# Moving the edge sums behind the slot's node and sort steps, and deepening the load buffers, in a two-layer graph attention kernel

## What is computed

```python
for l in range(L):                                   # L = 2
    xn = _layernorm(x, ln1_g[l], ln1_b[l])
    deg = segment_sum(ones, src); deg = (deg - deg.mean()) / (std(deg, ddof=1) + 1e-06)
    pos = xn @ Wpos[l] + bpos[l] + deg[:, None] * Wdeg[l][0] + bdeg[l]
    xp = xn + pos
    q, k, v = (xp @ W + b).reshape(n, H, HD)         # Wq, Wk, Wv
    att = clip(einsum('ehd,ehd->eh', q[dst], k[src]) / sqrt(HD), -50, 50)
    ex = exp(att - segment_max(att, dst)[dst]); s = segment_sum(ex, dst)
    aggr = segment_sum(v[src] * (ex / (s[dst] + 1e-16))[:, :, None], dst)
    x = x + (aggr @ Wo[l] + bo[l])
    h = gelu(_layernorm(x, ln2_g[l], ln2_b[l]) @ W1[l] + b1[l], approximate=False)
    x = x + (h @ W2[l] + b2[l])
return _layernorm(x_in + x)
```

## Time and profile before

| | |
|---|---|
| three runs | 3809.2 us median (3791.64 to 3824.87) |
| the profiled execution | 3805.99 us, of which 3804.0 us is the span of its instructions |
| mean granted TensorE clock | 0.886 of full speed |
| busy in the span | PE 83%, DVE 76%, POOL 66%, ACT 48% |
| indirect DMAs of POOL | 2448 |
| prologue; gathers of layer 0; of layer 1; rest | 0 to 289; 289 to 2074; 2126 to 3748; to 3804 us |

### The profile page before, as it was taken

How to read it: one execution, slowest core, us unless ns; L and a number is a source line. 1 busy time by engine, 2 the same in 40 slices (tenths; PEclk the granted TensorE clock), 3 DMA queues, 4 the chain that set the end, 5 groups by cost and what they waited for, 6 DMA issues and landing times.

```text
span 3804.0 us, 74324 instructions
## 1 busy us (share of the span) xinstructions
PE 3174.2 (83%) x25705; PEld 2515.7 (66%) x25705; DVE 2900.9 (76%) x6187; ACT 1820.2 (48%) x4404; POOL 2523.6 (66%) x2470
## 2 busy tenths in 40 slices
PE   4984688889898888889898688888888888888887
PEld 3763467667676676767676476667766676666665
DVE  8985688788678878877887387777877777777776
ACT  1331255445444444544555345555555555555555
POOL 1007777777666767766676477777777767777773
PEclk7685699999899999989999699899999989998997
DMA  3015455455454545545454355555555555555552
GB/s 85 22 62 150 115 159 173 151 158 152 139 153 148 161 144 155 154 142 150 148 176 133 102 164 160 178 165 166 151 178 168 167 165 168 168 168 165 163 168 79
DMA packets 427249, 558.53 MB, mean 147 GB/s; under 512 B 78473, under 2 KB 345441, under 8 KB 426677
## 3 DMA queue, kind: packets, MB, share of 16 engines
q0 software_dynamic: 117504, 321.02, 28.4%
q1 hardware_dynamic: 301862, 225.47, 19.6%
q10 hardware_dynamic: 7506, 7.20, 0.6%
HBM read 527.98 MB, written 25.44 MB: 145 GB/s over the span
## 4 chain that ended last, share of the span: by engine, by line
PE 44%; DVE 26%; issue 8%; ACT 8%; POOL 7%; DMA 5%; SPq 2%; DVEq 1%; POOLq 0%; ACTq 0%
PE psum L951 12%; POOL kv_ring L1964 6%; PE psum L1041 5%; DVE att L1682 4%; PE psum L992 4%; PE psum L1025 3%; DVE scratch L1673 3%; PE psum L1062 3%; DVE work L1377 2%; PE psum L1008 2%; DVE kv_ring L1394 2%; PE psum L1122 2%; DMA arena<-kv_table 2%; DVE arena L1724 2%; DMA q_win<-q_table 2%
## 5 line engine op out<-in xcount | busy, mean ns | idle before, releaser
L1964 POOL DMA_INDIRECT kv_ring<-kv_table,src_idx x1840 | 1888.1, 1026 | 746.5 <-issue 543.4
L1227 ACT ACTIVATE scratch<-psum 128x512 f32<-128x512 f32 (+1 forms) x1228 | 678.1, 567 | 484.1 <-PE psum L961 305.3
L1964 POOL DMA_INDIRECT arena<-kv_table,src_idx x608 | 617.2, 1015 | 241.0 <-issue 178.0
L951 PE MATMUL psum<-arena 128*128 128x256 f32 x2156 | 677.8, 437 | 72.5 <-ACT scratch L1227 42.1
L1238 ACT COPY arena<-psum 128x512 f32<-128x512 f32 x616 | 327.1, 532 | 593.7 <-PE psum L951 578.6
L992 PE MATMUL psum<-q_win,scratch 64*128 64x128 f32 x4896 | 413.1, 316 | 160.5 <-DVE scratch L1673 80.4
L951 PEld LDWEIGHTS psum<-arena 128*128 128x128 f32 x2156 | 425.7, 218 | 179.8 <-ACT scratch L1227 57.8
L1682 DVE TENSOR_REDUCE att<-scratch 128x64 f32<-128x1024 f32 (+1 forms) x460 | 535.7, 1165 | 0.1
L992 PEld LDWEIGHTS psum<-q_win,scratch 64*128 64x128 f32 x4896 | 349.2, 215 | 262.8 <-issue 165.6
L1673 DVE TENSOR_TENSOR scratch<-psum,kv_ring 128x1024 f32<-128x1024 f32 x230 | 280.4, 1219 | 154.7 <-DMA kv_ring<-kv_table,src_idx 92.2
L1008 PE MATMUL psum<-scratch 128*64 128x136 f32 x4896 | 371.5, 296 | 31.9 <-ACT work L1321 11.5
(11 more groups left out here) (252 smaller groups left out, 4839.3 us busy)
## 6 DMA issues: line engine op xcount, KB each, us to landing
arena<-kv_table SPq DMA_DIRECT2D x154, 896.0 KB
kv_ring<-kv_table,src_idx POOLq DMA_INDIRECT x1840
q_win<-q_table SPq DMA_DIRECT2D x612, 32.0 KB
work<-kv_table SPq DMA_DIRECT2D x98, 128.0 KB
q_win<-q_table SPq DMA_DIRECT2D x154, 64.0 KB
arena<-kv_table,src_idx POOLq DMA_INDIRECT x608
work<-q_table SPq DMA_DIRECT2D x98, 64.0 KB
kv_table<-work SPq DMA_DIRECT2D x49, 128.0 KB, 2.0
```

The source lines that it names most:

```text
L951: mm = e.matmul(to[:, t % 2 * 2 * D:(t % 2 + 1) * 2 * D], hot_source[:, t * P:(t + 1) * P], source_rows[:, t, :], start=True, stop=True)
L1227: e.activation(to[:, at:at + width], apart[k % FILL_BANKS][:, 0:width], ACT.Relu, bias=1.0, scale=-1.0).then_inc(apart_read, 1)
L1964: e.indirect_dma_start(kv[m % RING_KV][:, t, :], None, kv_table[l], bass.IndirectOffsetOnAxis(ap=src_idx[:, c * T + t:c * T + t + 1], axis ...
```

## The change

1. In DVE's program `add_sums` of u - 1 stands behind the node and sort steps of slot 2u + 1, and no longer straight behind the messages.
2. `q_win` has 4 buffers for 2, `source_rows` 2 for 1, `plan_b` 3 for 2. The loads are issued 4 units, two blocks and 6 units (`BLOCK_AHEAD`) ahead.
3. Fills: the first two `rows` of unit u + 3 stand in slot 2u + 1 and the last two of u + 2 in slot 2u, each half one slot sooner than before; `source` of u + 4 stands at the end of slot 2u + 1.
4. The 23 steps of a sort are laid evenly between the end of the sort before and the slot by which they must be done. Layer 0's blocks begin at chunk 19, for 17.
5. `b_next` becomes a part of the three-row bf16 split, so its PE product is one bf16 matmul of 3 rows for a float32 one of 1 row; the five DVE operations of the split work on 1280 columns, for 896.
6. The arena grows by 2240 words a partition, and `dynamic_dma_scratch_size=8192` is given at the build, for the default of 16384. This is the part of each SBUF partition that holds the descriptors of POOL's DMAs. Some semaphores are merged.

```diff
-FIRST_B = 17, 4
+FIRST_B = 19, 4
+QUERIES = 4
+BLOCK_AHEAD = 6
+PLANS_B = 3
-ARENA = 16656
+ARENA = 18896
...
         for u in range(self.nu):
-            ahead = [("source", u + 3, h) for h in range(2) if self.is_block(u + 3)]
+            ahead = [("source", u + 4, h) for h in range(2) if self.is_block(u + 4)]
             turn = [("turn", u + 2, h) for h in range(self.parts_of(u + 2))] if u + 2 < self.nu else []
             hot = [("hot", u, h) for h in range(self.parts_of(u))]
-            rows = [[("rows", u + 2, i)] if self.is_block(u + 2) else [] for i in range(4)]
-            fills[2 * u] = turn[:1] + rows[0] + turn[1:] + rows[1] + ahead
-            fills[2 * u + 1] = hot[:1] + rows[2] + hot[1:] + rows[3]
+            rows = [[("rows", u + (3 if i < 2 else 2), i)] if self.is_block(u + (3 if i < 2 else 2)) else [] for i in range(4)]
+            fills[2 * u] = turn[:1] + rows[2] + turn[1:] + rows[3]
+            fills[2 * u + 1] = hot[:1] + rows[0] + hot[1:] + rows[1] + ahead
...
     for s in range(NBS[0]) if l == 0 else range(NBS[0], NBS[1]):
-        if l == 0:
-            u = max(u, 2 * at[(s - 1) * OB] - 8 if s else 0)
-        else:
-            u = max(u, 2 * at[(s - NBS[0]) * 3 * OB])
+        first, end = u, 2 * (at[s * OB] - BLOCK_AHEAD) - 2
         for k in range(SORT_STEPS):
+            u = max(u, first + k * (end - first) // SORT_STEPS)
...
-            u += SORT_EVERY if s and 5 <= k < SORT_STEPS - 4 else 1
+            u += 1
...
-        q_win = sb("q_win", [P, 2, D])
+        q_win = sb("q_win", [P, QUERIES, D])
-        b_next = sb("b_next", [P, QKV])
+        b_next = sb("b_next", [3, QKV], BF16)
-        source_rows = part_of(TB * 2 * D).rearrange("p (t d) -> p t d", t=TB)
+        source_rows = [part_of(TB * 2 * D).rearrange("p (t d) -> p t d", t=TB) for _ in range(2)]
-        plan_b = part_of(TB * P).bitcast(BF16).rearrange("p (r e) -> p r e", r=2)
+        plan_b = part_of(PLANS_B * TB * P // 2).bitcast(BF16).rearrange("p (r e) -> p r e", r=PLANS_B)
...
-            if m >= 1:
-                e.wait_ge(apart_made, fill(block_unit(m - 1), "rows", 3) + 1)
+            if m >= 2:
+                e.wait_ge(apart_made, fill(block_unit(m - 2), "rows", 3) + 1)
...
-            if n >= 2:
-                e.wait_ge(spread, 2 * (n - 1))
+            if n >= QUERIES:
+                e.wait_ge(spread, 2 * (n - QUERIES + 1))
...
                     if slot % 2 == 0:
-                        if u + 2 < LAYERS[l].nu:
-                            load_queries(e, l, u + 2)
-                        if LAYERS[l].is_block(u + 1) and LAYERS[l].units[u + 1][1] + 1 < LAYERS[l].ub:
-                            load_sources(e, l, LAYERS[l].units[u + 1][1] + 1)
-                        if LAYERS[l].is_block(u + 4):
-                            load_block(e, l, LAYERS[l].units[u + 4][1])
+                        if u + QUERIES < LAYERS[l].nu:
+                            load_queries(e, l, u + QUERIES)
+                        if LAYERS[l].is_block(u + BLOCK_AHEAD):
+                            load_block(e, l, LAYERS[l].units[u + BLOCK_AHEAD][1])
+                    elif LAYERS[l].is_block(u + 2) and LAYERS[l].units[u + 2][1] + 2 < LAYERS[l].ub:
+                        load_sources(e, l, LAYERS[l].units[u + 2][1] + 2)
...
-                e.matmul(ps[:, 0:QKV], ones[0:1, :], b_next[0:1, :], start=True, stop=False)
+                e.matmul(ps[:, 0:QKV], ones_b[0:3, :], b_next[:], start=True, stop=False)
...
-                    elif slot % 2 == 1 and u <= LAYERS[l].nu:
-                        if u < LAYERS[l].nu:
-                            make_messages(e, l, u)
-                        if u >= 1:
-                            add_sums(e, l, u - 1)
+                    elif slot % 2 == 1 and u < LAYERS[l].nu:
+                        make_messages(e, l, u)
                     for j, k in at(slots, slot):
                         node_vector(e, l, j, k)
                     for s, k in at(SORTS[l], slot):
                         sort_vector(e, s, k)
+                    if slot % 2 == 1 and 1 <= u <= LAYERS[l].nu:
+                        add_sums(e, l, u - 1)
...
-    nc = _bacc.Bacc("TRN2", target_bir_lowering=False, num_devices=1)
+    nc = _bacc.Bacc("TRN2", target_bir_lowering=False, num_devices=1, dynamic_dma_scratch_size=8192)
```

More of the change, by code:

```diff
@@ L240 @@
 SORT_STEPS = 3 * SA + 11
-SORT_EVERY = 2
 def sort_steps(l):
@@ L257, in sort_steps @@
                 slots.setdefault(u + 1, []).append((s, -k))
-            u += SORT_EVERY if s and 5 <= k < SORT_STEPS - 4 else 1
-        assert u + 2 <= 2 * at[s * OB] - 8, (s, u, 2 * at[s * OB] - 8)
+            u += 1
+        assert u <= end + 1, (s, u, end)
     return [slots.get(u, []) for u in range(max(slots, default=-1) + 1)]
@@ L522, in graph_transformer @@
             semaphore(f"sort_{n}") for n in ("placed", "read", "dug", "out"))
-        bias_split, bias_in = semaphore("bias_split"), semaphore("bias_in")
-        block_in = [semaphore(f"block_in{i}") for i in range(2)]
-        rows_of_sources, rows_gathered = semaphore("rows_of_sources"), semaphore("rows_gathered")
+        bias_in = semaphore("bias_in")
+        block_in = [semaphore(f"block_in{i}") for i in range(PLANS_B)]
+        rows_of_sources = [semaphore(f"rows_of_sources{i}") for i in range(2)]
         gathered = [semaphore(f"gathered{i}") for i in range(RING_KV)]
@@ L528, in graph_transformer @@
         plan_ones = semaphore("plan_ones")
-        q_in = [semaphore(f"q_in{i}") for i in range(2)]
+        q_in = [semaphore(f"q_in{i}") for i in range(QUERIES)]
         apart_made, apart_read, spread = semaphore("apart_made"), semaphore("apart_read"), semaphore("spread")
@@ L630, in graph_transformer @@
         adds = [*itertools.accumulate(2 if chunk else 1 for chunk in of_chunk)]
-        q_loads = [sum(2 if of_chunk[m] else 1 for m in range(n % 2, n + 1, 2)) for n in range(units)]
+        q_loads = [sum(2 if of_chunk[m] else 1 for m in range(n % QUERIES, n + 1, QUERIES)) for n in range(units)]
         def count_width(s):
@@ L801, in sync_edges @@
                 slots = node_steps(l)
-                for u in range(2):
+                for u in range(QUERIES):
                     load_queries(e, l, u)
-                load_sources(e, l, 0)
+                for b in range(2):
+                    load_sources(e, l, b)
+                for u in range(BLOCK_AHEAD):
+                    if LAYERS[l].is_block(u):
+                        load_block(e, l, LAYERS[l].units[u][1])
                 for slot in range(slots_of(l)):
@@ L807, in sync_edges @@
                     if slot % 2 == 0:
-                        if u + 2 < LAYERS[l].nu:
-                            load_queries(e, l, u + 2)
-                        if LAYERS[l].is_block(u + 1) and LAYERS[l].units[u + 1][1] + 1 < LAYERS[l].ub:
-                            load_sources(e, l, LAYERS[l].units[u + 1][1] + 1)
-                        if LAYERS[l].is_block(u + 4):
-                            load_block(e, l, LAYERS[l].units[u + 4][1])
-                    elif u < LAYERS[l].nu and not LAYERS[l].is_block(u) and LAYERS[l].units[u][1] + ROWS < LAYERS[l].ca:
+                        if u + QUERIES < LAYERS[l].nu:
[4 more added lines that the diff above has]
+                        load_sources(e, l, LAYERS[l].units[u + 2][1] + 2)
+                    if slot % 2 == 1 and u < LAYERS[l].nu and not LAYERS[l].is_block(u) and LAYERS[l].units[u][1] + ROWS < LAYERS[l].ca:
                         load_plan(e, l, LAYERS[l].units[u][1] + ROWS)
@@ L992, in spread_chunk @@
                     m = e.matmul(q_edge[h][:, t * P:(t + 1) * P], hotT[n % 2][h * HALF:(h + 1) * HALF, t * P:(t + 1) * P],
-                                 q_win[h * HALF:(h + 1) * HALF, n % 2, :], start=True, stop=True)
+                                 q_win[h * HALF:(h + 1) * HALF, n % QUERIES, :], start=True, stop=True)
                     if t == T // 2 - 1:
@@ L1025, in spread_queries @@
                 m = e.matmul(q_edge[f % 2][:, (t - ts[0]) * P:(t - ts[0] + 1) * P], hotT[n % 2][:, t * P:(t + 1) * P],
-                             q_win[:, n % 2, :], start=True, stop=True)
+                             q_win[:, n % QUERIES, :], start=True, stop=True)
             m.then_inc(spread, 1)
@@ L1937, in pool_first @@
             e.memset(ones_b[:], 1.0).then_inc(pool_step, 1)
-            e.memset(places[:], 0.0).then_inc(places_empty, 1)
+            e.memset(places[:], 0.0).then_inc(pool_step, 1)
             e.wait_ge(pool_step, 10)
```

91 lines of the change are left out of this document (46 added, 45 removed).

## The result

The changed kernel takes 3682.4 us (median of 4 runs, 3681.2 to 3694.5) against 3815.8 us for the kernel before, measured beside it (median of 4, 3791.6 to 3824.9): a ratio of 0.9667 with a 95% interval of 0.9616 to 0.9719, 133 us or 3.3% faster. The forecast was 3697 us with a range of 3630 to 3780.

A forecast was written before the change was run, and what follows sets the result against it. POOL's gather pace was taken as a floor close below the present time, with the other engines holding it up. Terms -45 - 70 + 9 - 8 + 2 = -112 us took the 3809 us median to 3697, range 3630 to 3780.

The forecast's parts named there:

- The floor by POOL: Edge stages of both layers: POOL's own gather pace limits what quicker PE, DVE and ACT can win to 181 us.
- the first rival: POOL's floor reached in both layers, all its waits gone: 3615 us, chance 0.08.
- My upper end: Layer 0, 480 to 1900 us: POOL's floor of 1287 for 1420 us, PE at 91% with the clock at 0.97.
- the 181 us: POOL's waits for a free ring buffer, 133 us in layer 0 plus 48 in layer 1, taken as the most to win.
- add_sums behind the steps, even sorts: I take 70: Layer 0: later steps fill up to 144 us of DVE idle time; gain 70 us, between 24 and 133.
- the second rival: Layer 0 stays as it is, DVE's idle time at line 1729 being only where slack is counted: 3747 us, chance 0.13.
- in layer 0 loads hardly matter: Reading of the profile before: in layer 0 PE stops for single banks, such as 17.7 us for ACT's node step, not loads.
- Layer 1: loads: Layer 1: deeper query and source-row buffers remove 102 us of PE's load waits; gain 45 us, between 0 and 48.
- The prologue's +2: Before the first gather: the bias split's five DVE operations on 1280 columns for 896 cost 2 us.
- the end's -8: From the last gather to the kernel's end, 56 us: 8 us less, between 0 and 15, with the others closer behind POOL.
- The late bank: Edge stages of layer 0: PE waits for an edge bank freed later by the moved add_sums; 3843 to 3911 us, chance 0.07.
- The wait for descriptor memory: Gathers of both layers: POOL waits for the halved descriptor memory, +3% on each gather, 3789 us; chance 0.04.

The follow-up runs named there:

- the three made from it above: The changed kernel with one part taken back each: add_sums put back, 3689.6 us; loads of queries and source rows as before, 3718.8; fills as before, 3730.0.
- The halved messages above: The changed kernel with DVE making messages of each unit's first four tiles only: 5592.1 and 5570.2 us, with the kernel before at 5311.1 and 5261.7.

## Why the prediction was right, and where it was not

**The floor by POOL was right, but it was reached, which I held for unlikely.** The forecast said that POOL's pace is the floor and that PE would stay somewhat behind it in layer 0. It doesn't: 8.1 us of waits are left there, where 50 to 80 were expected, and 1.2 us in layer 1. What happened to POOL's waits is the first rival, to which I had given 0.08. Its argument against, that the stretch without stalls has no sort, did not hold: PE reached 91% at a clock of 0.95 with the sorts running. My upper end had just this, 91% at 0.97.

**That it still came out near 3697 and not at 3615 is a mis-sized term on each side.** First, the 181 us were too large a ceiling. Each of the 80 waits contains the 0.30 us that POOL leaves between any two gathers, so only 181 - 80 x 0.30 = 157 us could be won. Second, the gathers became longer. They take 2549.3 us in all (1922.9 + 626.4) for 2505.3 before, +44 us, nearly all of it in layer 0 (mean 1054 ns for 1023; in layer 1 1028 for 1024). For layer 0: 133.2 us in 50 waits, less the gaps, is 118 us, of which 6 are left; -112 + 40 = -72, against the table's -72.7. For layer 1, in the same way, -39 + 4 = -35, against its -34.6. Had the gathers kept their length, the kernel would have come out near 3640 us, an estimate from these 44 us. So the mechanism, POOL as a floor, was right, while that the number fits within 15 us is in part luck: more of the waits went than forecast, and the gathers gave some of it back.

**Why they became longer.** Above the median, and without the first one, the gathers have 183 us in the kernel before and 225 us in the changed one. Set beside DVE's instructions by start and duration, nearly all of this lies in the gathers that overlap a message multiply (line 1697, later 1704): 172 us in 667 gathers before, 217 us in 756 after. The other gathers, 1780 and 1691, have 12 and 8 us; those beside the product with k, a multiply of the same size that reads one operand from PSUM, have none. The time for which a gather and a message run at once grew from 349 to 413 us, since POOL no longer stands still during the messages. At 0.49 us of excess for each us of overlap, as before, this gives some 32 of the 42 us; after the change it is 0.53, and why is open. The halved messages above support that these all-SBUF multiplies are the cause. The rise in layer 0 is larger than what traces differ by: its gathers take 1285 and 1295 us in the kernel before and with `add_sums` moved alone, and 1316 to 1326 us in the changed kernel and the three made from it above. In layer 1 they take 1206 and 1221 us against 1222 to 1245, a spread as large as the difference, so the +4 there says little. The halved descriptor memory was never tried alone, but the median of 946 ns didn't move, and neither did the gathers away from the messages. The Trainium skill ("SBUF — State Buffer", section "Who interferes with whom") says that a DMA that seems to stall beside a DVE operation was one of POOL's, kept from its descriptors, and that a probe saw this beside a copy but not beside a `tensor_tensor`. This trace agrees as to the direction, but not on the second point: DVE's message is a TENSOR_TENSOR, and its 1.2 us cost the gathers beside it about 0.5 us. The same section of the Trainium skill also has a DVE instruction with two inputs in SBUF contend with a GpSimd instruction that reads SBUF, as a gather does its indices; that would fit, but no run here separates the two.

**The step that failed is the cause given for layer 0.** It was "add_sums behind the steps, even sorts: I take 70". The amount (61 net of the blocks' later start) is close to the 73 measured; the cause isn't. Alone the move took 17 us from POOL's 133, and taken away it gave back 15. I had read 144.0 us of idle time of DVE as time to be won, although the same view showed that DVE waits at the next product as well, and the second rival named exactly this. In its place stands the order of the fills, which I had put down to layer 1: 55 us of waits in layer 0 and next to nothing in layer 1. The move of `add_sums` and the fills together don't explain all of the 125 us: with the old fills, but all else changed, 63 us are left of 133, and `add_sums` alone gives 17 of these 70. That leaves some 50 us for the sorts, the bias product, the later blocks and the block's plan, or for parts that only pay together; which of them is open. The plan I had passed over: PE's second largest wait in layer 0 was for it, from 480 to 2074,

```profile
PE psum L939 <- DMA arena<-sorted_table: 15.2, 23, 1.5
```

and in the changed kernel, with its third plan buffer, this wait is gone. So "in layer 0 loads hardly matter" was not quite right either; no run took that buffer back.

**Layer 1: loads.** Right in cause and near in amount, 34.6 for 45: POOL's waits fell by 46.8 us, but 8 of these are the gaps in them, and the gathers became 4 us longer. The detail that the fill-bank waits would shrink was wrong; they rose from 85.6 us (45.5 + 40.1) to 116.0 us (94.7 + 21.3, quoted above) and cost next to nothing, POOL's waits in this layer being 1.2 us.

**The small terms.** The bias product fell from 47.4 us of PE over the kernel to 16.8, somewhat more than worked out for layer 0 (40.8 to 18):

```profile
L1136 PE MATMUL psum<-b_next,ones_b 3*128 3x384 bf16 x49 | 16.8, 344 | 6.4 <-ACT work L1341 4.6 <-ACT work L1349 1.7
```

The prologue's +2 was +1.0, the end's -8 was -11.3. The gap between the layers fell by 6.8 us, for which I had no term. I take it for the same effect as at the end, the others being closer behind POOL when the last gather is out; no run tests this. The late bank did come, but small. PE's waits from 480 to 2000 of the changed kernel:

```profile
PE psum L1015 <- DVE arena L1731: 14.7, 12, 2.0
...
PE psum L1115 <- DVE arena L1731: 6.9, 3, 2.4
...
PE psum L1094 <- DVE arena L1731: 6.2, 5, 2.0
```

Over all its lines PE waits 31 us there for DVE's line 1731 (`add_sums` of a chunk), where it waited 4 us for it before and 4 again with `add_sums` put back. "In tens of us" was my sign for this rival, so the mechanism is real, at 0.14 us for each of layer 0's units instead of 0.6. It did not set the time, since POOL waited only 8 us in layer 0. The wait for descriptor memory did not show.

## What to carry to other kernels

Idle time in front of an in-order engine's instruction is only worth what the next wait behind it leaves: before it is counted as a gain, look at where the engine stands next. Where a queue with a fixed pace (here 2448 gathers at 1.25 us) has little slack, count what it loses to others, less the gap it always leaves, as the ceiling of any change to the others; and expect it to lose a little again, since it now works beside operations during which it used to stand. In a schedule by hand, try the order of the fillers by itself: here taking it back cost 48 us, more than taking back the load buffers (36), though only the latter had shown up as a list of waits on one cause. When one wait line falls, look at the other lines of the same engine before calling it gained.

## What the runs showed of the hardware

- A gather of 128 rows takes a median of 946 ns, with 16 or 8 KiB of descriptor memory, and 0.30 us lie between two.
- A gather that overlaps DVE's float32 multiply with all operands in SBUF takes longer, by 0.49 to 0.53 us for each us of overlap (172 us over 349, 217 us over 413); gathers beside the multiply that reads one operand from PSUM take no longer. With the multiplies halved the excess fell from 65 to 19 us.
- The granted clock was 0.92 and 0.93 in the long stretches of the two layers before and 0.95 and 0.96 after; over the kernel PE's time without work fell from 630 to 585 us.
